# A spectral block on one core: TensorE's block order in the MLP slices, layer-2 chunks by twos and x's transposes moved to the inverse transform

## The chip, the cores and the metric

The kernel runs on one core of one Trainium2 chip. The metric is the device time in microseconds of one execution. Everything is float32. TensorE does the matrix products and the transpositions (a transposition is a matmul too), VectorE (DVE), ScalarE (ACT) and GpSimd (POOL) do the elementwise work, SyncE (SP) issues all DMAs.

## The reference, cut to what matters

The input x is 16 images of 56 x 56 positions with 64 channels. Two layers follow each other:

```
layer 0: whitening
  m, cov of the 64 channels over all 50,176 positions
  L = cholesky((1-eps) cov + eps I);  y = inv(L) (x - m) * gamma + beta
layer 1: residual = y
  h  = layer_norm(y) * g1 + b1
  xf = rfft2(h over rows and columns)
  o1 = relu(complex 8-block linear of xf);  o2 = softshrink(complex 8-block linear of o1, 0.01)
  r  = irfft2(o2) + h + residual
  n2 = layer_norm(r)
  out = gelu(n2 @ mw1 + mb1) @ mw2 + mb2 + r        (64 -> 256 -> 64 channels)
```

The Fourier transforms are done as matrix products with cosine and sine tables. Softshrink is computed as v - clamp(v, -0.01, 0.01).

## The kernel before, in words

The kernel first reads all images for the covariance and factors it. Then it goes through the images in eight pairs, one outer step each. Two images fill 112 of 128 partitions (2 x 56 rows).

A step i works on three pairs at once. For pair i it does the spectral part: dft_h, dft_w, layer_1, layer_2 (eight chunks), inv_w (the inverse column transform, eight chunks) and inv_h. For pair i-1 it does the MLP in seven slices of 8 columns. For pairs i+1 and i+2 it does the whitening and the transposes of x. The work of the last two is spread by hand among the rest; there is no planner, and each engine has its own program, kept in step with the others by semaphores. Step 0 has no MLP beside it (`behind` is false), steps 6 and 7 have no x to transpose (`ahead2` is false), and step 7 has no next pair (`ahead` is false). After step 7 comes the MLP of the last pair.

One slice of TensorE's program is `mlp(i, s, fill)` at line 1091. It calls mlp_in(s) (64 to 256 channels, line 1069), mlp_out(s-1) (256 to 64, line 1078), then fill(0), fill(1), transpose_n(s+1) (the n2 transposes, line 1060), fill(2), turn_out(s-1) (the MLP output turned back, line 1087), fill(3). The fills bring in the spectral work: in slices 1 and 2 the chunks 0 to 3 and 4 to 7 of layer_2 (line 1023), in slices 3 and 4 those of inv_w (line 1034). The table `X_BESIDE` says which of the seven blocks of x's transposes (line 953) follow which fill.

PSUM bank 3 (`BANK_M`) is used in turn by mlp_out(s-1), transpose_n(s+1) and turn_out(s-1). ScalarE empties it after the first two (ev_mlp_t, ev_n2), VectorE after the third: `ev_mlp` at line 701 reads the bank, adds the residual and writes `oslice`, line 707, which SP then stores. So the mlp_out of the next slice waits in `free_c` until ev_mlp is done.

Layer-2 chunks use banks 1 and 2 in turn. For each chunk VectorE adds the bias (line 692) and clamps (line 698), and POOL subtracts the two (line 436), with two buffers between VectorE and POOL. VectorE's slice_ at line 730 calls e0, e1, e2, then ev_mlp(s-1), then e3. In slices 1 and 2 the e's are the chunks, with the statistics of the next pair's layer norm behind some of them, seven bn_stats at a time (line 588): in slice 1 behind the second and the fourth chunk, in slice 2 behind the first, the second and the fourth. In slices 3 and 4 the e's hold the rest of that layer norm.

Slices 5 and 6 are not calls of mlp: in the tail of a step mlp_in(5), mlp_out(4), inv_h, transpose_n(6), turn_out(4), mlp_in(6) and mlp_out(5) are written out by hand. `mlp_order` (line 112) lists the use of the banks for the semaphore counts and has to follow the order of the calls.

Of the kernel before, what the change touches and what calls it, by code (L numbers as in the profile page):

```python
# [79 lines left out]

X_BESIDE = {1: [[0], [], [1], []], 2: [[2], [], [3], []], 3: [[4], [5], [6], []]}


def x_bank(i, k):
# [25 lines left out]
def mlp_order(i):  # L112

    order = [("n2", 0), ("n2", 1)] if last_pair(i) else [("n2", 0)]
    for s in range(SLICES):
        order += [("hid", s, m, v) for m in range(2) for v in range(2)]
        if last_pair(i):
            order += [("out", s - 2)] * (s > 1) + [("mlp", s - 1)] * (s > 0) + [("n2", s + 2)] * (s < SLICES - 2)
        else:
            order += [("mlp", s - 1)] * (s > 0) + [("n2", s + 1)] * (s < SLICES - 1) + [("out", s - 1)] * (s > 0)  # L120
    if last_pair(i):
        return order + [("mlp", SLICES - 1), ("out", SLICES - 2), ("out", SLICES - 1)]
    return order + [("mlp", SLICES - 1), ("out", SLICES - 1)]
# [44 lines left out]
def build(nc, x, consts, params, out):  # L168
# [5 lines left out]
    with ExitStack() as ctx:  # L174
# [151 lines left out]
        with nc.Block() as block:  # L326
# [123 lines left out]
            def _(dve):  # L450
# [279 lines left out]
                def step(i, ahead, behind):  # L730
                    def slice_(s, e0, e1, e2, e3):

                        e0()
                        e1()
                        e2()
                        if behind and s > 0:
                            ev_mlp(i - 1, s - 1)
                        e3()

                    def next_(what, *args):  # L740
                        if ahead:
                            what(i + 1, *args)

                    if behind:
                        ln2_stats(i - 1, 4)
                        if i > 1:
                            ev_mlp(i - 2, SLICES - 1)
                        for k in range(5, 8):
                            ln2_stats(i - 1, k)
                        ln2(i - 1)  # L750
                    next_(ev_whiten, [1] if behind else [0, 1])
                    ev_layer_1(i)
                    if i == 0:
                        folded_weights()
                    slice_(0, lambda: next_(ev_whiten, [2, 3, 4]), lambda: next_(ev_whiten, [5]),
                           lambda: next_(ev_whiten, [6]), lambda: next_(ln1_stats, [0]))
                    slice_(1, lambda: ev_layer_2(i, [0]), lambda: (ev_layer_2(i, [1]), next_(ln1_stats, [1])),
                           lambda: ev_layer_2(i, [2]), lambda: (ev_layer_2(i, [3]), next_(ln1_stats, [2])))
                    slice_(2, lambda: (ev_layer_2(i, [4]), next_(ln1_stats, [3])),
                           lambda: (ev_layer_2(i, [5]), next_(ln1_stats, [4])),  # L760
                           lambda: ev_layer_2(i, [6]), lambda: (ev_layer_2(i, [7]), next_(ln1_stats, [5])))
                    slice_(3, lambda: next_(ln1_stats, [6, 7]), lambda: next_(mean_rstd, 0),
                           lambda: next_(ln1_subtract, 0), lambda: None)
                    slice_(4, lambda: next_(ln1_rstd, 0), lambda: next_(ln1_subtract, 1), lambda: None,
                           lambda: next_(ln1_rstd, 1))
                    slice_(5, lambda: ev_inv_h(i, [0, 1]), lambda: None, lambda: ev_inv_h(i, [2, 3]), lambda: None)
                    if ahead:
                        slice_(6, lambda: ev_inv_h(i, [4, 5]), lambda: (ln2_stats(i, 0), ln2_stats(i, 1)),
                               lambda: ev_inv_h(i, [6, 7]), lambda: (ln2_stats(i, 2), ln2_stats(i, 3)))
# [44 lines left out]
            def _(pe):  # L814
# [213 lines left out]
                def inv_w(i, ks):  # L1028
                    for k in ks:

                        pe.wait_ge(y_ready, i * 8 + 4 * (k // 4) + 4)
                        t = free_b(i, INVW + k)
                        for j in range(4):
                            last = nc.tensor.matmul(t[:, j * 112:j * 112 + 112], y_v[:, 4 * k + j, :], cc("invw"),  # L1034
                                                    start=True, stop=True)
                        last.then_inc(pe_b, 1)
# [54 lines left out]
                def mlp(i, s, fill):  # L1091

                    mlp_in(i, s)
                    if s > 0:
                        mlp_out(i, s - 1)
                    fill(0)
                    fill(1)
                    if s < SLICES - 1:
                        transpose_n(i, s + 1)
                    fill(2)  # L1100
                    if s > 0:
                        turn_out(i, s - 1)
                    fill(3)

                def step(i, ahead, ahead2, behind):

                    def slice_(s, fill):
                        if behind:
                            mlp(i - 1, s, fill)
                        else:  # L1110
                            for j in range(4):
                                fill(j)

                    def whiten_next(j):
                        if ahead and j < 3:
                            whiten(i + 1, [4 + j])

                    def and_x(s, what):
                        def both(j):
                            what(j)  # L1120
                            if ahead2:
                                transpose_x(i + 2, X_BESIDE[s][j])
                        return both

                    dft_h(i)
                    if ahead:
                        whiten(i + 1, [0])
                    dft_w(i)
                    if ahead:
                        whiten(i + 1, [1])  # L1130
                    layer_1(i)
                    if i == 0:
                        folded_weights()
                    if ahead:
                        whiten(i + 1, [2])

                    pe.wait_ge(b_act, i * B_ACT + b_done("act", L2 - 1))
                    pe.wait_ge(b_dve, i * B_DVE + b_done("dve", L2 - 1))
                    if behind:
                        transpose_n(i - 1, 0)  # L1140
                    if ahead:
                        whiten(i + 1, [3])
                    slice_(0, whiten_next)
                    slice_(1, and_x(1, lambda j: layer_2(i, j)))
                    slice_(2, and_x(2, lambda j: layer_2(i, 4 + j)))
                    slice_(3, and_x(3, lambda j: inv_w(i, [j])))
                    slice_(4, lambda j: inv_w(i, [4 + j]))
                    if behind:
                        mlp_in(i - 1, 5)
                        mlp_out(i - 1, 4)  # L1150
                    inv_h(i, 0)
                    if behind:
                        transpose_n(i - 1, 6)
                    inv_h(i, 1)
                    if behind:
                        turn_out(i - 1, 4)
                        mlp_in(i - 1, 6)
                    inv_h(i, 2)
                    if behind:
                        mlp_out(i - 1, 5)  # L1160
                    if not ahead:
                        turn_out(i - 1, 5)
                        mlp_out(i - 1, 6)
                    inv_h(i, 3)
                    if behind:
                        turn_out(i - 1, 5 if ahead else 6)
# [34 lines left out]
            def _(act):  # L1201
# [94 lines left out]

                def mlp(i, s, fill):

                    gelu(i, s, 0)
                    gelu(i, s, 1)  # L1300
                    if s > 0:
                        ev_mlp_t(i, s - 1)
                    fill(0)
                    fill(1)
                    if s < SLICES - 1:
                        ev_n2(i, s + 1)
                    fill(2)
                    fill(3)

                def step(i, ahead2, behind):  # L1310
# [7 lines left out]
                    def x_next(s, j):  # L1318
                        if ahead2:
                            ev_x(i + 2, X_BESIDE[s][j])  # L1320

                    def first_inv_w(j):
                        ev_inv_w(i, [j])
                        x_next(3, j)

                    ev_dft_h(i)
                    ev_dft_w(i)
# [4 lines left out]
                    slice_(1, lambda j: x_next(1, j))  # L1332
                    slice_(2, lambda j: x_next(2, j))
                    slice_(3, first_inv_w)
                    slice_(4, lambda j: ev_inv_w(i, [4 + j]))
                    slice_(5, lambda j: None)
                    slice_(6, lambda j: None)

# [168 lines left out]
```

## Time and profile before

| | |
|---|---|
| median of 3 runs | 841.62 us (840.57 to 844.27) |
| profiled execution, its own time | 842.9 us |
| its span, first to last instruction | 841.1 us |
| mean granted TensorE clock | 0.932 |
| TensorE busy | 778.3 us (93%) |
| VectorE busy | 569.4 us (68%) |
| ScalarE busy | 378.4 us (45%) |
| GpSimd busy | 251.9 us (30%) |

Busy shares are averages over the whole span. In the rows below a block of equal instructions is merged to one line; the time from the start of one block to the start of the next is what a block takes, since a matmul's recorded end overlaps the next one. In brackets stands the idle time of the engine just before the block, with the instruction whose end released it.

### The profile page before, as it was taken

How to read it: one execution, taken by the hardware profiler on the slowest of the kernel's cores; microseconds unless marked ns; L12 is line 12 of the kernel's file. 1: busy time of each engine (PE TensorE's matmuls, PEld its weight loads, DVE VectorE, ACT ScalarE, POOL GpSimd, SP SyncE). 2: the span in 40 equal slices, each digit the busy share in tenths (PEclk: the TensorE clock that was granted, in tenths of full speed). 3: DMA queues.
4: the chain of work that ended last, by engine and by line, in shares of the span. 5: the costliest groups of instructions: out<-in, count | busy, mean ns of one | idle time of the engine just before them, and what ended most of it. 6: DMA issues, size and time to landing. Idle time of an engine off the chain costs nothing.

```text
span 841.1 us, 17115 instructions
## 1 busy us (share of the span) xinstructions
PE 778.3 (93%) x6823; PEld 542.9 (65%) x6823; DVE 569.4 (68%) x1860; ACT 378.4 (45%) x687; POOL 251.9 (30%) x107
## 2 busy tenths in 40 slices
PE   7999996986799999999999999999999998989987
PEld 5985555875477667666766667676757664746433
DVE  4567777279577767776776777677867695843551
ACT  0011005623164735563556455545554545455455
POOL 4000000932903270427042604360435045413000
PEclk9895557899699999999999999999999999999999
DMA  9943002002000121002100300030001001001012
GB/s 263 276 113 107 1 0 75 3 2 78 1 1 13 34 65 46 24 23 82 29 25 23 95 17 24 23 108 4 23 23 34 2 24 34 23 2 34 23 34 67
DMA packets 10369, 39.41 MB, mean 47 GB/s; under 512 B 1282, under 2 KB 1410, under 8 KB 8834
## 3 DMA queue, kind: packets, MB, share of 16 engines
q1 hardware_dynamic: 10290, 38.31, 15.8%
q8 instruction: 55, 0.90, 0.4%
q14 instruction: 24, 0.20, 0.1%
HBM read 25.46 MB, written 12.85 MB: 46 GB/s over the span
## 4 chain that ended last, share of the span: by engine, by line
PE 80%; DVE 15%; issue 3%; ACT 1%; DMA 0%; DVEq 0%; ACTq 0%
PE psum L1069 11%; PE psum L1078 10%; PE psum L982 7%; PE psum L1047 6%; PE psum L992 6%; PE psum L1023 6%; PE psum L1034 6%; PE psum L1007 6%; PE psum L966 5%; PE psum L829 4%; PE psum L886 4%; DVE stats L588 3%; PE psum L1087 3%; PE psum L953 2%; PE psum L1060 2%
## 5 line engine op out<-in xcount | busy, mean ns | idle before, releaser
L1271 ACT ACTIVATE hid<-psum,hbias 128x448 f32<-128x448 f32 x224 | 124.0, 636 | 80.6 <-PE psum L1069 80.6
L436 POOL TENSOR_TENSOR p_y<-layer,clamped 128x512 f32<-128x512 f32 x64 | 75.5, 1180 | 240.1 <-DVE clamped L698 240.1
L1069 PE MATMUL psum<-n2T,mw1s 64*128 64x448 f32 x448 | 102.7, 577 | 1.7 <-ACT n2T L1264 1.7
L1078 PE MATMUL psum<-hid,prm 128*64 128x448 f32 x448 | 96.3, 552 | 2.0 <-DVE oslice L707 2.0
L401 POOL TENSOR_TENSOR hbuf<-hbuf,prm 112x3584 f32<-112x3584 f32 x7 | 43.4, 6205 | 111.1 <-DVE hbuf L653 111.1
L1047 PE MATMUL psum<-u_r,cst 58*112 58x448 f32 x256 | 60.4, 592 | 15.5 <-DVE rbuf L720 11.3
L1023 PEld LDWEIGHTS psum<-w2s,o_g 128*64 128x64 f32 x1856 | 60.1, 138 | 15.5 <-issue 8.9
L692 DVE TENSOR_TENSOR layer<-psum,prm 128x512 f32<-128x512 f32 x64 | 40.4, 631 | 41.6 <-PE psum L1023 41.6
L1034 PEld LDWEIGHTS psum<-cst,p_y 128*128 128x128 f32 x512 | 61.2, 192 | 11.2 <-issue 5.6
L1023 PE MATMUL psum<-w2s,o_g 128*64 128x64 f32 x1856 | 66.3, 224 | 2.1 <-DVE layer L692 2.1
L1034 PE MATMUL psum<-cst,p_y 128*128 128x112 f32 x512 | 66.7, 277 | 1.2 <-DVE layer L692 1.2
L982 PE MATMUL psum<-cst,hbuf 112*112 112x116 f32 x512 | 57.1, 270 | 9.5 <-DVE hbuf L802 7.4
L672 DVE TENSOR_TENSOR ybuf<-psum,prm 112x512 f32<-112x512 f32 x49 | 33.9, 691 | 46.4 <-PE psum L966 45.8
L982 PEld LDWEIGHTS psum<-cst,hbuf 112*112 112x112 f32 x512 | 54.3, 182 | 16.6 <-issue 9.0
L1078 PEld LDWEIGHTS psum<-hid,prm 128*64 128x64 f32 x448 | 27.3, 136 | 58.4 <-issue 42.8
L966 PE MATMUL psum<-wy,xT 128*112 128x128 f32 x448 | 61.0, 287 | 3.8 <-DVE ybuf L672 3.0
L588 DVE BATCH_NORM_STATS2 stats<-ybuf 112x6 f32<-112x64 f32 x448 | 60.6, 212 | 3.7 <-ACT ybuf L1354 3.5
L966 PEld LDWEIGHTS psum<-wy,xT 128*112 128x112 f32 x448 | 54.7, 186 | 13.1 <-issue 13.1
L1214 ACT COPY u_r<-psum 112x464 f32<-112x464 f32 x64 | 35.0, 546 | 60.0 <-PE psum L982 60.0
L1069 PEld LDWEIGHTS psum<-n2T,mw1s 64*128 64x128 f32 x448 | 39.9, 190 | 30.1 <-issue 21.6
L992 PE MATMUL psum<-cst,u_r 112*128 112x116 f32 x464 | 53.3, 275 | 0.6 <-ACT u_r L1214 0.6
L1047 PEld LDWEIGHTS psum<-u_r,cst 58*112 58x112 f32 x256 | 23.2, 184 | 46.2 <-issue 45.3
(130 smaller groups left out, 1308.7 us busy)
## 6 DMA issues: line engine op xcount, KB each, us to landing
xin<-x_dram SPq DMA_DIRECT2D x8, 1568.0 KB, 8.3
out_dram<-oslice SPq DMA_DIRECT2D x56, 224.0 KB, 2.2
ybuf<-x_dram SPq DMA_DIRECT2D x2, 1568.0 KB, 16.8
fbuf<-x_dram SPq DMA_DIRECT2D x2, 1568.0 KB, 19.9
xin<-x_dram SPq DMA_DIRECT2D x4, 392.0 KB, 5.2
n<-x_dram SPq DMA_DIRECT2D x1, 1568.0 KB, 22.1
n<-x_dram SPq DMA_DIRECT2D x4, 392.0 KB, 15.7
prm<-params_dram SPq DMA_DIRECT2D x1, 742.0 KB, 3.9
```

Of the source, the lines that this page charges most:

```text
L436: nc.gpsimd.tensor_tensor(yk, a, b, ALU.subtract).then_inc(y_ready, 1)
L588: last = nc.vector.bn_stats(stats[:, w, :], src[:, w * C:(w + 1) * C])
L966: last = nc.tensor.matmul(t[0:ROWS, j * 128:(j + 1) * 128], xT[:, w * ROWS:(w + 1) * ROWS], wy[:], start=(i > 0), stop=True, skip_group_ch ...
L982: last = nc.tensor.matmul(t[0:ROWS, j * 2 * KR:(j + 1) * 2 * KR], h_w[:, 4 * k + j, :], cc("f1", ROWS), start=True, stop=True)
L992: last = nc.tensor.matmul(t[:, j * 4 * KF:(j + 1) * 4 * KF], u_r[0:ROWS, (4 * k + j) * 128:(4 * k + j + 1) * 128], cc("f2", ROWS), start=T ...
L1007: one = nc.tensor.matmul(t[b][:, 0:(z - a) * KF], w1s[C * b:C * b + C, 256 * s + 128 * half:256 * s + 128 * half + 128], p_v[C * b:C * b + ...
L1023: last = nc.tensor.matmul(t[C * r:C * r + C, j * C:j * C + C], o_g[:, at:at + C], w2s[:, 128 * half + C * r:128 * half + C * r + C], start ...
L1034: last = nc.tensor.matmul(t[:, j * 112:j * 112 + 112], y_v[:, 4 * k + j, :], cc("invw"), start=True, stop=True)
L1047: one = nc.tensor.matmul(t[d][0:ROWS, 0:7 * C], cc("invh")[rows, ROWS * m:ROWS * m + ROWS], g[rows], start=(m == 0), stop=(m == 1))
L1069: nc.tensor.matmul(t[:, 0:4 * ROWS], mw1s[C * v:C * v + C, HH * m:HH * m + HH], n2T[C * v:C * v + C, s % 2, :], start=True, stop=True).the ...
L1078: last = nc.tensor.matmul(t[C * v:C * v + C, 0:4 * ROWS], pp("mw2")[:, C * m:C * m + C], hid[:, s % 2, m, v, :], start=(m == 0), stop=(m = ...
L1271: nc.scalar.activation(hid[:, s % 2, m, v, :], bank[CH_MLP[i].bank[k]][:, 0:4 * ROWS], ACT.Gelu, bias=hbias[:, m:m + 1]).then_inc(c_act, 1)
```

## The change

The change moves instructions; it adds and removes none.

- `X_BESIDE`: the seven blocks of x's transposes were in slices 1, 2 and 3 (two, two and three of them). Now one is in slice 1, one in slice 2, three in slice 3 and two in slice 4. Within a fill an x block now comes ahead of the fill's other work instead of behind it.
- TensorE, slices 1 and 2: turn_out(s-1) comes behind fill(3) instead of ahead of it. With the emptied table entries the order of a slice is mlp_in, mlp_out, chunk, chunk, n2 transposes, x transposes, chunk, chunk, turn_out. VectorE's ev_mlp(s-1) moves behind e3 to match.
- The tail: mlp_out(4) comes ahead of mlp_in(5), and ScalarE's ev_mlp_t(4) ahead of the gelus of slice 5; `mlp_order` follows.

```
-X_BESIDE = {1: [[0], [], [1], []], 2: [[2], [], [3], []], 3: [[4], [5], [6], []]}
+X_BESIDE = {1: [[], [], [0], []], 2: [[], [], [1], []], 3: [[2], [], [3], [4]], 4: [[5], [], [6], []]}
...
 # VectorE, slice_
                         e2()
+                        if s in (1, 2):
+                            e3()
                         if behind and s > 0:
                             ev_mlp(i - 1, s - 1)
-                        e3()
+                        if s not in (1, 2):
+                            e3()
...
 # TensorE, mlp
                     fill(2)
+                    if s in (1, 2):
+                        fill(3)
+                        turn_out(i, s - 1)
+                        return
                     if s > 0:
                         turn_out(i, s - 1)
                     fill(3)
...
                         def both(j):
-                            what(j)
                             if ahead2:
                                 transpose_x(i + 2, X_BESIDE[s][j])
+                            what(j)
...
-                    slice_(4, lambda j: inv_w(i, [4 + j]))
+                    slice_(4, and_x(4, lambda j: inv_w(i, [4 + j])))
                     if behind:
+                        mlp_out(i - 1, 4)
                         mlp_in(i - 1, 5)
-                        mlp_out(i - 1, 4)
...
 # ScalarE, mlp
+                    if s == 5:
+                        ev_mlp_t(i, s - 1)
                     gelu(i, s, 0)
                     gelu(i, s, 1)
-                    if s > 0:
+                    if s not in (0, 5):
                         ev_mlp_t(i, s - 1)
...
 # ScalarE, step
                     def first_inv_w(j):
+                        x_next(3, j)
                         ev_inv_w(i, [j])
-                        x_next(3, j)
+
+                    def last_inv_w(j):
+                        x_next(4, j)
+                        ev_inv_w(i, [4 + j])
```

## Rows read from the trace of the kernel before

**Rows 1.** The page's chain that ended last, shares of the span by engine.
```profile
PE 80%; DVE 15%; issue 3%; ACT 1%; DMA 0%; DVEq 0%; ACTq 0%
```

**Rows 2.** TensorE's timeline (start us, length us, instructions), step 4, slices 1 and 2.
```profile
505.45 1.10 PE L1023 MATMUL psum<-w2s,o_g 128*64 128x64 f32 x32
...
509.71 0.60 PE L953 MATMUL psum<-cst,xin 112*128 112x112 f32 x4
510.15 0.60 PE L1087 MATMUL psum<-cst,mlp_t 128*112 128x128 f32 x4
...
511.42 1.77 PE L1069 MATMUL psum<-n2T,mw1s 64*128 64x448 f32 x8
513.12 1.72 PE L1078 MATMUL psum<-hid,prm 128*64 128x448 f32 x8
514.67 1.10 PE L1023 MATMUL psum<-w2s,o_g 128*64 128x64 f32 x32
```

**Rows 3.** TensorE's timeline, step 4, slices 3 and 4 and the tail's start.
```profile
522.34 1.72 PE L1078 MATMUL psum<-hid,prm 128*64 128x448 f32 x8
...
531.52 1.72 PE L1078 MATMUL psum<-hid,prm 128*64 128x448 f32 x8
...
536.33 0.60 PE L1087 MATMUL psum<-cst,mlp_t 128*112 128x128 f32 x4
...
537.74 1.77 PE L1069 MATMUL psum<-n2T,mw1s 64*128 64x448 f32 x8
```

**Rows 4.** VectorE's timeline, step 4, slices 1 to 4.
```profile
506.60 0.69 DVE L692 TENSOR_TENSOR layer<-psum,prm 128x512 f32<-128x512 f32 x1 [2.52 <-PE psum L1023]
507.32 0.43 DVE L698 TENSOR_SCALAR clamped<-layer 128x512 f32<-128x512 f32 x1
...
...
522.33 2.75 DVE L588 BATCH_NORM_STATS2 stats<-ybuf 112x6 f32<-112x64 f32 x21
...
530.55 0.68 DVE L707 TENSOR_TENSOR oslice<-psum,fbuf 112x512 f32<-112x512 f32 x1
...
536.96 0.69 DVE L707 TENSOR_TENSOR oslice<-psum,fbuf 112x512 f32<-112x512 f32 x1 [1.86 <-PE psum L1087]
```

**Rows 5.** VectorE's and POOL's timelines, step 0, layer-2 chunks and statistics.
```profile
182.23 0.68 DVE L692 TENSOR_TENSOR layer<-psum,prm 128x512 f32<-128x512 f32 x1
...
187.39 1.10 DVE L698 TENSOR_SCALAR clamped<-layer 128x320 f32<-128x320 f32 x1
...
189.31 0.67 DVE L692 TENSOR_TENSOR layer<-psum,prm 128x512 f32<-128x512 f32 x1
...
195.79 2.74 DVE L588 BATCH_NORM_STATS2 stats<-ybuf 112x6 f32<-112x64 f32 x21
...
187.04 1.28 POOL L436 TENSOR_TENSOR p_y<-layer,clamped 128x512 f32<-128x512 f32 x1 [0.67 <-DVE clamped L698]
```

**Rows 6.** TensorE's timeline, step 6, and VectorE's last write-back before the wait.
```profile
671.20 2.03 PE L1023 MATMUL psum<-w2s,o_g 128*64 128x64 f32 x64
673.17 0.60 PE L1060 MATMUL psum<-cst,n 112*128 112x112 f32 x4
...
695.97 1.72 PE L1078 MATMUL psum<-hid,prm 128*64 128x448 f32 x8 [1.78 <-DVE oslice L707]
...
695.23 0.68 DVE L707 TENSOR_TENSOR oslice<-psum,fbuf 112x512 f32<-112x512 f32 x1
```

**Rows 7.** TensorE in the last MLP; the windows row is length, busy, granted clock, DMA.
```profile
810.60 0.60 PE L1060 MATMUL psum<-cst,n 112*128 112x112 f32 x4 [2.37 <-DVE n L631]
811.13 3.18 PE L1069 MATMUL psum<-n2T,mw1s 64*128 64x448 f32 x8
...
811.00:813.00 2.00, 2.00 (x9) 0.59 0.00 0
```

**Rows 8.** VectorE's write-back and TensorE's mlp_out behind it, step 7, slices 1 and 2.
```profile
756.94 0.67 DVE L707 TENSOR_TENSOR oslice<-psum,rbuf 112x512 f32<-112x512 f32 x1
...
758.02 1.72 PE L1078 MATMUL psum<-hid,prm 128*64 128x448 f32 x8
```

More of the change, by code:

```diff
@@ L115, in mlp_order @@
     for s in range(SLICES):
+        if s == 5 and not last_pair(i):
+            order += [("mlp", 4)]
         order += [("hid", s, m, v) for m in range(2) for v in range(2)]
@@ L119, in mlp_order @@
         else:
-            order += [("mlp", s - 1)] * (s > 0) + [("n2", s + 1)] * (s < SLICES - 1) + [("out", s - 1)] * (s > 0)
+            order += [("mlp", s - 1)] * (s not in (0, 5)) + [("n2", s + 1)] * (s < SLICES - 1) + [("out", s - 1)] * (s > 0)
     if last_pair(i):
@@ L1334, in step @@
                     slice_(3, first_inv_w)
-                    slice_(4, lambda j: ev_inv_w(i, [4 + j]))
+                    slice_(4, last_inv_w)
                     slice_(5, lambda j: None)
```

## The prediction, made before the result was known

> **What bounds the kernel now.** I read the page first, then TensorE's instructions in order of time, then VectorE's, then TensorE's granted clock by windows. The chain that ended last is 80% TensorE and 15% VectorE [rows 1], so what counts is TensorE's order and each place where it waits. I call a pass of the outer loop a step. Steps 1 to 5 repeat each other to a hundredth of a microsecond, 82.88 us apart; the rows are of step 4. In its slices 1 to 4 TensorE doesn't wait at all [rows 2, 3]. Step 6 has no x to transpose: there the same TensorE work is shorter, VectorE's is not, and mlp_out of slice 3 waits 1.78 us for VectorE's write-back `oslice` [rows 6]. That is the wait to watch. mlp_out writes bank 3, which the previous slice's out transposes used too, so it needs the VectorE read of that bank (ev_mlp) to be over.
>
> **Slices 1 and 2, TensorE.** All x transposes but one per slice go, and the rest of the order is mlp_in, mlp_out, chunk, chunk, n2, x, chunk, chunk, turn_out. Spacings, start to start: two adjacent chunks 1.97 us (step 6, [rows 6]); a transposition block before another 0.44 (510.15 - 509.71), a transposition block and the short last chunk together 1.27 (511.42 - 510.15), mlp_in 1.70 [rows 2]. Turn_out straight before mlp_in isn't in the rows; it lies between the 0.44 and its recorded length of 0.60, I take 0.53. From the first chunk to the point where the next mlp_out could start: 1.97 (two chunks) + 0.44 (n2) + 1.27 (x and the last chunk) + 0.98 (the third chunk) + 0.53 + 1.70 = 6.9 us. Before it was 513.12 - 505.45 = 7.67. So TensorE alone would gain 0.77 us a slice.
>
> **Slices 1 and 2, VectorE.** What is moved here is more than TensorE's blocks. turn_out(s-1) now comes after the fourth chunk, and ev_mlp(s-1) in VectorE's queue after e3, which is the last chunk's add and clamp and then seven statistics. Before, ev_mlp stood ahead of e3, and turn_out ahead of the last chunk. Now mlp_out of the next slice waits for all of it. The chunk's add starts 1.15 us after its matmuls start [rows 2, 4]. From there on VectorE has work without a break, and step 0 shows exactly this sequence, since it has no ev_mlp in it [rows 5]: from the first add of slice 1 to the first add of slice 2 it is 189.31 - 182.23 = 7.08 us. ev_mlp then takes its place at the end, and mlp_out starts 0.74 us after ev_mlp starts [rows 6]. Slice 1: 1.15 + 7.08 + 0.74 = 8.97 us against 7.67: 1.30 later, with a TensorE wait of 8.97 - 6.9 = 2.1 us. Slice 2 has two more groups of statistics between the chunks: 195.79 - 189.31 = 6.48 to the statistics of e3, 0.90 for seven of them (a third of that row's 21), so 1.15 + 6.48 + 0.90 + 0.74 = 9.27 against 522.34 - 514.67 = 7.67: 1.60 later, a wait of 2.4 us.
>
> The 7.08 holds an effect that step 4 didn't have: a clamp that starts while POOL subtracts lasts until POOL has finished. The clamp of 320 columns at 187.39 took 1.10 us beside POOL's subtraction of 187.04 to 188.32 [rows 5]; the full clamp of 512 columns at 507.32 took 0.43 [rows 4]. With chunks far apart the clamps fell between the subtractions, with chunks by twos they don't. In the Trainium skill, SBUF — State Buffer, section "SBUF: two separate sides", the port pair of VectorE and GpSimd is an exclusive lock held for a whole instruction. By that rule, the trace agrees; without it three clamps a step would be some 0.6 us shorter each, which is a rival below.
>
> **Slices 3 and 4.** Slice 3 has three x blocks before and after; I take nothing for it. VectorE is not late there: from the statistics at 522.33 to ev_mlp at 530.55 it is 8.22 us [rows 4], 0.90 less now that seven statistics are over before ev_mlp(1), 0.68 more for ev_mlp itself, 8.0 against TensorE's 531.52 - 522.34 = 9.18 [rows 3]. Slice 4 gets two x blocks that had been in slices 1 and 2: 2 x 0.44 = +0.88 us, uncovered, since TensorE is the bound there. This is the point of the balance: x's transposes leave a stretch where VectorE decides the end and go to one where TensorE does.
>
> **Tail.** mlp_out(4) now stands ahead of mlp_in(5), so it lacks the 1.70 us that covered ev_mlp(3). That starts at 536.96, 0.63 after turn_out, so the bank is free 0.63 + 0.74 = 1.37 after turn_out starts; TensorE gets there after 537.74 - 536.33 = 1.41 [rows 3, 4]. It just fits: 0, with up to 0.1 a step on top. ScalarE's turned order there and x's later copies to xT (needed a step later) cost nothing: ScalarE is busy 45% of the span by the page. SP's queue doesn't change its order, and the next load of x stands behind stores that come later than the moved blocks.
>
> **Sum.** Steady step: +1.30 + 1.60 + 0 + 0.88 = +3.78, five times: +18.9. Step 0: its slices 1 to 4 are VectorE's already, and TensorE waits later for it anyway: 0. Step 6, first chunk to mlp_out of slice 3: 8.97 + 1.55 (mlp_out to chunk, [rows 2]) + 9.27 + 7.98 (9.18 less three x blocks, about 1.2) = 27.77 against 695.97 - 671.20 = 24.77: +3.0; here the old 1.78 us wait is used up by the new ones. Step 7 has no statistics: ev_mlp comes later by the last chunk's add, about 0.5 (0.69 for a full one, [rows 4]), and its held clamp, 189.31 - 187.39 less the 0.90 of statistics = 1.02 [rows 5], 1.5 in all, of which 758.02 - 756.94 - 0.74 = 0.34 was slack [rows 8]: +1.2 in each of two slices, +2.4. Together +24.3 us.
>
> **TensorE's clock.** The new waits are 2.1 and 2.4 us in five steps, 2.5 and 2.8 in step 6: twelve that are over 2 us. At 810.60 a single wait of 2.37 us stood behind a busy stretch, and the clock fell: 0.59 in the next 2 us, the lower of the two levels (1.2 GHz) for most of it, and an mlp_in took 3.18 us instead of 1.77 [rows 7]. After the wait of 1.78 us at 695.97 the next block was at full speed, 1.72 [rows 6]. The new waits lie between and above. A fall costs 3.18 - 1.77 = 1.4 us in that block and a little in its neighbour; I estimate 1.5. It counts in full, for what follows each wait (mlp_out and the first chunk) starts VectorE's next sequence. The bounds are 0 and 12 x 1.5 = 18; I take 10 of 12, since the nearest row to 2.4 us is the one that fell: +15.
>
> The Trainium skill speaks against this: TensorE: Matmul & The Clock Gate, "Part 1: The HAM clock gate", has the clock fall after an idle stretch that is longer than each of the new waits. By it the time would be that of the first rival; the fall behind 2.37 us in this trace is against it.
>
> So +24.3 + 15 = +39.3 on the profiled execution's 842.9 us (span 841.1): 882.2. That execution lies 1.3 above the median of 841.62, so **881 us**.
>
> **Rivals.**
> 1. The same waits, but the clock stays up, as behind 1.78 us: 841.6 + 24.3 = 866. Against it stands the fall after 2.37. Chance 0.20.
> 2. The clamps aren't held, since POOL's subtractions fall otherwise, and then the waits are shorter and end at full clock: three clamps x 0.6 = 1.8 less in five steps, about 1.2 less each in steps 6 and 7: 866 - 11.2 = 855. For it: in step 4 they weren't held. Chance 0.05.
> 3. The other side: ev_mlp is in time, TensorE never waits for it, and the grouping pays. Then a steady step is 2 x (6.9 + 1.55 - 9.22) + 0.88 = -0.66, step 6 loses its wait too (22.5 against 24.77, -2.3), step 7 -0.2: -5.8 in all, 836. It decides by one gap: ev_mlp must be over by the end of the next mlp_in, 2.2 us after the last chunk lands (0.53 + 1.70); the add, clamp and statistics ahead of it and itself come to over 2.5 even from an idle VectorE. Chance 0.05.
> 4. All twelve waits bring a fall and some of them two stretches of low clock in succession, as the low clock lasted through step 0's tail: 892 to 905. Chance 0.08.
>
> **Numbers.** My forecast, between eight and all twelve falls, 873 to 891, has 0.62. The range takes in the first rival: 862 to 892. About 0.5% (4 us) is what a measurement can tell from no change: faster 0.05 (rival 3), within it 0.02, slower 0.93.
>
> **What would show it.** Right: mlp_out waits of 2 to 3 us with `oslice` as their releaser, in slices 2 and 3 of steps 1 to 6, some 1.3 in step 7; clamps of 1.0 to 1.1 us in steps 1 to 5; granted clock at one half behind most of the waits; slice 4 longer by 0.9; ev_mlp right behind e3's statistics. Wrong: no such waits (rival 3), waits at full clock (rival 1), clamps of 0.43 (rival 2), or a new wait in the tail before mlp_out(4).

## The result, and the profile after

The changed kernel took 862.14 us (median of 4 runs, 861.28 to 863.51) against 842.94 for the kernel before beside it (4 runs, 840.57 to 846.08): a ratio of 1.024, 95% interval 1.021 to 1.027, so 2.4% slower. The profiled execution took 861.5 us with a span of 859.7, 18.6 over the span before. I had forecast 881, with 862 to 892 as the range: the direction is right, but the slowdown is about half of what I forecast. The time lies 0.1 us inside the range's lower edge, next to my first rival ("the same waits, but the clock stays up", 866) and outside my forecast proper (873 to 891).

The page of the changed kernel: the chain of waits by engine, which answers to [rows 1], and mlp_out's group (busy us, mean ns, idle us just before and its releaser):
```profile
PE 70%; DVE 23%; issue 5%; POOL 1%; ACT 1%; DMA 0%; DVEq 0%; ACTq 0%
...
L1083 PE MATMUL psum<-hid,prm 128*64 128x448 f32 x448 | 96.9, 554 | 28.8 <-DVE oslice L709 28.8
```
TensorE's share of the chain fell from 80% to 70% and VectorE's rose from 15% to 23%. TensorE is idle for 28.8 us in front of mlp_out, released by the write-back `oslice`: 14 waits, two in each of steps 1 to 7. Before there were two such waits in the whole program, the 1.78 us of [rows 6] the longer.

TensorE's timeline of the changed kernel, step 4 (start us, length us, instructions, [idle before <- releaser]), which answers to [rows 2, 3]:
```profile
513.88 2.04 PE L1028 MATMUL psum<-w2s,o_g 128*64 128x64 f32 x64
515.84 0.60 PE L1065 MATMUL psum<-cst,n 112*128 112x112 f32 x4
516.28 0.55 PE L958 MATMUL psum<-cst,xin 112*128 112x112 f32 x4
516.76 1.74 PE L1028 MATMUL psum<-w2s,o_g 128*64 128x64 f32 x52
518.42 0.65 PE L1092 MATMUL psum<-cst,mlp_t 128*112 128x128 f32 x4
519.00 1.77 PE L1074 MATMUL psum<-n2T,mw1s 64*128 64x448 f32 x8
522.83 1.73 PE L1083 MATMUL psum<-hid,prm 128*64 128x448 f32 x8 [2.06 <-DVE oslice L709]
524.39 2.04 PE L1028 MATMUL psum<-w2s,o_g 128*64 128x64 f32 x64
...
533.65 1.72 PE L1083 MATMUL psum<-hid,prm 128*64 128x448 f32 x8 [2.34 <-DVE oslice L709]
...
542.70 1.72 PE L1083 MATMUL psum<-hid,prm 128*64 128x448 f32 x8
...
549.65 1.72 PE L1083 MATMUL psum<-hid,prm 128*64 128x448 f32 x8
551.31 1.77 PE L1074 MATMUL psum<-n2T,mw1s 64*128 64x448 f32 x8
```
The order is the new one: two chunks in one block (x64), n2 and x, two chunks (x52, the last is short), turn_out, mlp_in. The first wait is 2.06 us, the second 2.34; slice 3 to slice 4 has none, and neither has the tail. The mlp_outs shown are mlp_out(1), (2), (3) and (4) at 522.83, 533.65, 542.70 and 549.65; each stands at the start of the slice behind its own. "mlp_out of slice 3", here and in the prediction, is mlp_out(3).

VectorE's timeline of the same slice, which answers to [rows 4], and POOL's subtraction beside its last clamp:
```profile
515.02 0.69 DVE L694 TENSOR_TENSOR layer<-psum,prm 128x512 f32<-128x512 f32 x1 [2.52 <-PE psum L1028]
...
516.81 1.01 DVE L700 TENSOR_SCALAR clamped<-layer 128x512 f32<-128x512 f32 x1
...
520.20 1.10 DVE L700 TENSOR_SCALAR clamped<-layer 128x320 f32<-128x320 f32 x1
521.22 0.97 DVE L590 BATCH_NORM_STATS2 stats<-ybuf 112x6 f32<-112x64 f32 x7
522.11 0.67 DVE L709 TENSOR_TENSOR oslice<-psum,fbuf 112x512 f32<-112x512 f32 x1
...
519.85 1.27 POOL L438 TENSOR_TENSOR p_y<-layer,clamped 128x512 f32<-128x512 f32 x1 [0.67 <-DVE clamped L700]
```
From 515.02 VectorE works without a break until the write-back at 522.11, which mlp_out waits for; it starts 0.72 us after it. Two clamps in this slice take over 1.0 us; the last of them ends at 521.30, 0.2 us behind POOL's subtraction (519.85 + 1.27 = 521.12).

Now the clock. TensorE alone, windows of 6 us (length, busy, granted clock, DMA share, GB/s): one ahead of step 0's chunks, which the table below needs, and three from mlp_outs that had waited:
```profile
174.00:180.00 6.00, 4.43 (x48) 1.00 0.00 0
435.55:441.55 6.00, 6.00 (x80) 0.72 0.13 40
522.83:528.83 6.00, 6.00 (x132) 1.00 0.13 38
619.82:625.82 6.00, 6.00 (x34) 0.72 0.13 38
```
Behind the wait that ends at 522.83 the clock stays at 2.4 GHz. Of the windows behind the twelve new waits it fell to 1.2 GHz for part of two only: behind the first wait of step 3 and the second of step 5. The timeline shows the price there: at 437.39 the two chunks took 3.33 us, in place of 2.04.

Where the span's 18.6 us are, by the start of the first layer-2 chunk of each step:

| stretch | before | after | difference |
|---|---|---|---|
| start to step 1 | 256.82 | 254.24 | -2.58 |
| step 1 to 6, steps without a fall | 82.88 each | 86.18 each | +3.30 each, +16.5 |
| extra in the steps 3 and 5, with a fall | | 87.27, 87.77 | +2.7 |
| step 6 | 80.22 | 81.68 | +1.46 |
| step 7 to the end | 89.7 | 90.2 | +0.5 |

The first row isn't the change's: another execution of the changed kernel reached step 1 at 256.72, and over the twelve profiles of this case the start lies between 252.1 (experiment 6) and 257.6, with low stretches of TensorE's clock at other places (174 to 180 us: 1.00 here, 0.72 in the execution of before). The step-to-step distances are free of that, so the experiments are read by them.

### The profile page after: what moved, and what is told of

The parts are those of the page before. It is cut to its first block, busy times and chain, and to the rows that moved or that the text cites. A ratio compares the mean times of both kernels' runs of the same rounds, so it can differ in the third digit from the quotient of the medians.

```text
span 859.7 us, 17115 instructions
## 1 busy us (share of the span) xinstructions
PE 772.0 (90%) x6823; PEld 542.4 (63%) x6823; DVE 581.2 (68%) x1860; ACT 376.5 (44%) x687; POOL 251.6 (29%) x107
## 4 chain that ended last, share of the span: by engine, by line
PE 70%; DVE 23%; issue 5%; POOL 1%; ACT 1%; DMA 0%; DVEq 0%; ACTq 0%
PE psum L1083 10%; PE psum L1074 8%; PE psum L987 7%; PE psum L997 6%; PE psum L1039 6%; PE psum L1052 6%; DVE stats L590 6%; PE psum L1012 5%; PE psum L971 5%; DVE layer L694 4%; PE psum L834 3%; PE psum L891 3%; DVE clamped L700 2%; PE psum L1092 2%; PE psum L958 2%
## 5 line engine op out<-in xcount | busy, mean ns | idle before, releaser
L1083 PE MATMUL psum<-hid,prm 128*64 128x448 f32 x448 | 96.9, 554 | 28.8 <-DVE oslice L709 28.8
L1052 PE MATMUL psum<-u_r,cst 58*112 58x448 f32 x256 | 58.2, 574 | 14.5 <-DVE rbuf L722 10.3
L1289 ACT ACTIVATE mlp_t<-psum,prm 128x448 f32<-128x448 f32 x56 | 35.5, 634 | 71.1 <-PE psum L1083 69.6
L1028 PE MATMUL psum<-w2s,o_g 128*64 128x64 f32 x1856 | 62.8, 227 | 3.6 <-DVE layer L694 3.6
```

The lines of the kernel that those rows point to most:

```text
L1028: last = nc.tensor.matmul(t[C * r:C * r + C, j * C:j * C + C], o_g[:, at:at + C], w2s[:, 128 * half + C * r:128 * half + C * r + C], start ...
L1052: one = nc.tensor.matmul(t[d][0:ROWS, 0:7 * C], cc("invh")[rows, ROWS * m:ROWS * m + ROWS], g[rows], start=(m == 0), stop=(m == 1))
L1083: last = nc.tensor.matmul(t[C * v:C * v + C, 0:4 * ROWS], pp("mw2")[:, C * m:C * m + C], hid[:, s % 2, m, v, :], start=(m == 0), stop=(m = ...
```

## The experiments

**1. The change with VectorE's write-back put back ahead of e3** (and nothing else different). This is the one edit that my working made responsible.
```
-                        if s in (1, 2):
-                            e3()
                         if behind and s > 0:
                             ev_mlp(i - 1, s - 1)
-                        if s not in (1, 2):
-                            e3()
+                        e3()
```


> The changed kernel with VectorE's ev_mlp(s-1) back ahead of e3 in slices 1 and 2; TensorE's new order and x's new places stay. Theory (VectorE's order makes the waits): the waits of 2.06 and 2.34 us before mlp_out of slices 2 and 3 go. TensorE needs 6.9 + 1.55 us for each of slices 1 and 2 (before 9.22), VectorE's write-back is ready at 6.1 + 0.74 = 6.8. In slice 3 VectorE is now late instead, by some 0.7 us, for its layer-norm chain from chunk 4 to the write-back is 15.9 + 0.74 = 16.6 against TensorE's 16.0. Per steady step -0.77 -0.77 -0.13 +0.67 +0.73 -0.17 = -0.4, in all 2 to 3 us below the kernel before: about 840. Rival (the blocks by twos and x among the inverse transform cost by themselves): the time stays at 855 or more.

Measured 835.5 us (834.2 to 837.2), ratio 0.991 [0.988, 0.995]; step 82.36. TensorE's timeline of this kernel, slice 2 and the mlp_out of slice 3:
```profile
509.87 2.03 PE L1025 MATMUL psum<-w2s,o_g 128*64 128x64 f32 x64
...
516.73 1.72 PE L1080 MATMUL psum<-hid,prm 128*64 128x448 f32 x8
...
526.50 1.72 PE L1080 MATMUL psum<-hid,prm 128*64 128x448 f32 x8 [0.64 <-DVE oslice L709]
```
The first chunk to mlp_out is 516.73 - 509.87 = 6.86 us, my TensorE sum of 6.9, with no wait. One line of VectorE's order makes 3.82 of the 86.18 us of a step, and turns a kernel 2.4% slower into one 0.9% faster. Of that 0.9% the new order itself has only a part: of the 8.6 us between this execution's span (832.5) and that of before (841.1), 2.6 are the five steady steps'; 2.4 lie ahead of step 1, which differs between executions anyway, and 1.5 in step 6 and 2.1 in step 7 and the last MLP, mostly from falls of the clock that lie otherwise. What is left is a wait of 0.64 us in slice 3, where VectorE is now late.

**2. The other way round: the kernel before, with only that order changed.**
```
+                        if s in (1, 2):
+                            e3()
                         if behind and s > 0:
                             ev_mlp(i - 1, s - 1)
-                        e3()
+                        if s not in (1, 2):
+                            e3()
```


> The kernel before with one edit: VectorE's ev_mlp(s-1) behind e3 in slices 1 and 2. TensorE's order, x's places and the tail are those of before. Theory: each of the two slices ends with VectorE's add, clamp, seven statistics and write-back behind the last chunk, mlp_out waits some 1.6 us twice a steady step: +16 in five steps, +3 in step 6, +2 in step 7, about 864, the whole loss of the changed kernel and more. Rival (TensorE's new order is what costs): 843 to 846.

Measured 861.5 us (859.7 to 864.1), ratio 1.022 [1.019, 1.026]; step 85.76. TensorE's timeline of this kernel, step 4, and the longest wait of step 6:
```profile
514.62 1.10 PE L1026 MATMUL psum<-w2s,o_g 128*64 128x64 f32 x32
...
523.57 1.72 PE L1081 MATMUL psum<-hid,prm 128*64 128x448 f32 x8 [1.22 <-DVE oslice L707]
...
695.07 2.74 PE L1081 MATMUL psum<-hid,prm 128*64 128x448 f32 x8 [2.29 <-DVE oslice L707]
```
The order alone brings +2.88 us a step, nearly all of the change's +3.30. First chunk to mlp_out is 523.57 - 514.62 = 8.95 us, the same as in the changed kernel: VectorE's sequence sets it whichever way TensorE's blocks lie, and the wait is shorter (1.22, 1.52) only because more of TensorE's work fills the slice. From the first add to the write-back it is 7.09 us here too. VectorE does idle in between, 0.46 and 0.19 us for chunks that come later, but its second and last clamp start later beside POOL's subtractions and end just behind them all the same: they take 0.46 and 0.81 us in place of 1.01 and 1.10. Behind the wait at 695.07 the clock fell, and mlp_out took 2.74 us.

**3 and 4. The x transposes alone, and the tail alone**, each in the kernel before. The first is the new `X_BESIDE` with what reads it, the second puts mlp_out(4) ahead of mlp_in(5).
```
-X_BESIDE = {1: [[0], [], [1], []], 2: [[2], [], [3], []], 3: [[4], [5], [6], []]}
+X_BESIDE = {1: [[], [], [0], []], 2: [[], [], [1], []], 3: [[2], [], [3], [4]], 4: [[5], [], [6], []]}
```


> The kernel before with x's transposes in their new places (one, one, three and two in slices 1 to 4, each ahead of the fill's work), and nothing else. Theory: slices 1 and 2 shorten by about 0.7 us each since VectorE's write-back is in time at 6.5 to 6.8 us, slice 4 lengthens by 0.7, and slice 3 gets a wait of about 0.6 for the write-back behind VectorE's layer-norm chain: -0.2 a step, 840 to 843. Rival (x's two blocks in slice 4 are a pure loss, and slices 1 and 2 don't gain): +0.7 a step, 846 to 847.

```
+        if s == 5 and not last_pair(i):
+            order += [("mlp", 4)]
...
-                        mlp_in(i - 1, 5)
                         mlp_out(i - 1, 4)
+                        mlp_in(i - 1, 5)
```


> The kernel before with only the tail's part of the change: mlp_out(4) ahead of mlp_in(5), ScalarE's ev_mlp_t(4) ahead of the gelus of slice 5. To be read from the distance of one step's first layer-2 chunk to the next one's (82.88 us in the kernel before). Theory (from the changed kernel's trace, where the tail was 0.17 us shorter): 82.7, since mlp_in ahead of inv_h takes less than mlp_out does, and ev_mlp(3) is just in time. Rival (the cover of 1.70 us is missing, as bounded in the prediction): a wait before mlp_out(4) of up to 0.1, 82.9 to 83.0.

The first took 842.8 us (839.5 to 844.5), ratio 1.000 [0.998, 1.002], step 82.69: -0.19. It has a wait of 0.50 us in slice 3: TensorE leaves slices 1 and 2 earlier, and VectorE comes no sooner. The second took 842.6 us (one execution); its step is 82.69 too, -0.19, without a new wait. So neither is to blame, and each gives back a little. With experiment 1 the grouping of the chunks is worth 82.36 - 82.88 + 0.38 = -0.14 a step, if the three add up (no run has the grouping alone). Slice 3's wait, 0.50 here and 0.64 in experiment 1, is in these values.

**5. The change, with e3's seven statistics moved behind the write-back.**
```
                         if s in (1, 2):
                             e3()
                         if behind and s > 0:
                             ev_mlp(i - 1, s - 1)
+                        if s in (1, 2):
+                            next_(ln1_stats, [2 if s == 1 else 5])
```


> The changed kernel with the seven statistics of e3 moved behind ev_mlp in slices 1 and 2; the last chunk's add and clamp stay ahead of it. Theory (the wait is the sum of what stands ahead of the write-back in VectorE's queue): each of twelve waits shortens by the 0.89 us of seven statistics, 2.06 to 1.17 and 2.34 to 1.44; step 7 stays as it is: -10.7, about 851.5. Rival (the wait is set by POOL's subtraction or by ScalarE): unchanged at 862.

Measured 852.8 us (851.4 to 854.4), ratio 1.011 [1.007, 1.015]; step 84.40. TensorE's timeline of this kernel, the two mlp_outs of step 4 that wait:
```profile
518.66 1.72 PE L1085 MATMUL psum<-hid,prm 128*64 128x448 f32 x8 [1.17 <-DVE oslice L709]
...
528.58 1.72 PE L1085 MATMUL psum<-hid,prm 128*64 128x448 f32 x8 [1.45 <-DVE oslice L709]
```
Each wait is shorter by the 0.89 us that the statistics take, and the step by twice that (1.78). What stands between the last chunk's add and the write-back goes into the time one for one. None of its waits for the write-back was followed by a fall of the clock.

**6. The change, with POOL's subtraction cut short** (64 columns in place of 512), to free VectorE's clamps from it. This kernel leaves out the rest of the softshrink.
```
-    nc.gpsimd.tensor_tensor(yk, a, b, ALU.subtract)
+    nc.gpsimd.tensor_tensor(yk[:, 0:1], a[:, 0:1], b[:, 0:1], ALU.subtract)
```


> The changed kernel with POOL's subtraction cut to one of up to eight columns' groups of each chunk (the rest of the shrunk sum is left out), so POOL is done with each chunk in about 0.2 us and not 1.3. Nothing waited for the subtraction's end by itself. Theory (a clamp that starts while POOL subtracts is held until POOL ends): the three clamps of 1.0 to 1.1 us a step take 0.43 and 0.51, the waits shrink by 1.17 in slice 1 (2.06 to 0.9) and 0.59 in slice 2 (2.34 to 1.75), -11 in steps 1 to 6 and -2 to -3 in step 7, about 848. Rival (these clamps are slow for another reason, such as the order of VectorE's own instructions): clamps and time unchanged, 862.

Measured 841.5 us (841.1 to 846.7), ratio 1.001 [0.999, 1.003]; step 84.07. VectorE's and POOL's timelines of this kernel, step 4, slice 1:
```profile
507.23 0.43 DVE L700 TENSOR_SCALAR clamped<-layer 128x512 f32<-128x512 f32 x1
...
510.04 0.33 DVE L700 TENSOR_SCALAR clamped<-layer 128x320 f32<-128x320 f32 x1
...
507.74 0.33 POOL L438 TENSOR_TENSOR p_y<-layer,clamped 128x64 f32<-128x64 f32 x1 [0.73 <-DVE clamped L700]
```
The clamps are 0.43 and 0.33 us in place of 1.01 and 1.10, and the waits 0.71 and 1.56: shorter by 1.35 = 0.58 + 0.77, and by 0.77. Two thirds of a first wait are the time in which VectorE is held by POOL. The Trainium skill has VectorE and GpSimd share a port pair as an exclusive lock for a whole instruction (SBUF — State Buffer, "SBUF: two separate sides"); by that rule a clamp that starts beside a subtraction can't end before it, and here the trace agrees, 1.10 with it and 0.33 without. The time is 6.5 us below what I expected here. Of the 20.1 us between the two profiled spans (859.7 and 839.6) 10.6 are the five steady steps', 2.7 the falls that went, 2.1 step 6, 2.6 step 7 and the end, and 2.1 lie ahead of step 1 (252.1 us), where step 0 has held clamps too [rows 5] and the clock was low for less time. I had counted neither the falls nor step 0.

**7. The change with longer waits**: seven more statistics, written to a spare tile, ahead of the write-back in slices 1 and 2.
```
+                        if ahead and behind:
+                            for w in range(7):
+                                nc.vector.bn_stats(spare[:, i, at + w, :], ybuf[:, w * C:(w + 1) * C])
```


> The changed kernel with seven more statistics (of columns that are not needed, into a spare tile) ahead of the write-back in slices 1 and 2 of steps 1 to 6. The twelve waits grow by 0.89 to 2.95 and 3.2 us. Without the clock: +10.7, 873. Theory on the clock (the longer the wait, the surer the fall; 2.1 to 2.3 us is near the edge, so two of twelve fell): most of the twelve are followed by a stretch of low granted clock, +10 to +15 more, 880 to 888. Rival (a fall depends on where a wait lies in time, not on its length): again two or three falls, 873 to 877.

Measured 882.3 us (882.1 to 882.5, two runs), ratio 1.048 [1.044, 1.051]. TensorE alone, windows of 6 us behind the first and the second wait of step 1, and the mlp_out of a wait in step 3:
```profile
264.46:270.46 6.00, 6.00 (x132) 1.00 0.14 41
276.16:282.16 6.00, 6.00 (x34) 0.72 0.13 38
...
443.51 2.97 PE L1089 MATMUL psum<-hid,prm 128*64 128x448 f32 x8 [2.94 <-DVE oslice L710]
```
The waits are 2.8 to 3.3 us long, and now the clock falls behind 8 of 12. They also lie at other times than before, so the length isn't the only thing that differs.

**8. The changed kernel again, unaltered**, to see whether the falls keep their places.

> The changed kernel, unaltered, once more. Both theories: 862 and waits of 2.06 and 2.33 us. If what comes before a wait in the program decides whether the clock falls, the falls stand where they stood: behind the first wait of step 3 and the second of step 5. If it is the wait's place in time against something that doesn't keep step with the program, they stand elsewhere, and their number can differ.

It took 865.0 us (two runs), ratio 1.027 [1.024, 1.031]. The falls came in the same two places. TensorE's timeline of this execution:
```profile
438.01 2.17 PE L1083 MATMUL psum<-hid,prm 128*64 128x448 f32 x8 [2.06 <-DVE oslice L709]
439.96 3.23 PE L1028 MATMUL psum<-w2s,o_g 128*64 128x64 f32 x64
...
622.40 2.23 PE L1083 MATMUL psum<-hid,prm 128*64 128x448 f32 x8 [2.33 <-DVE oslice L709]
```
Two executions are few, but it speaks for something in the program's course, and against chance, as what picks the waits.

**9. The best version: experiment 1, with slice 3's write-back put ahead too** (of e2), where experiment 1 had its 0.64 us.
```
+                        if s == 3 and behind:
+                            ev_mlp(i - 1, s - 1)
                         e2()
-                        if behind and s > 0:
+                        if behind and s > 0 and s != 3:
                             ev_mlp(i - 1, s - 1)
```
(Experiment 1's edit is in it as well.)

> The changed kernel with VectorE's ev_mlp ahead of e3 in slices 1 and 2, and in slice 3 also ahead of the layer norm's first subtraction (e2). In slice 3 turn_out(2) is there before VectorE's chain of small operations ends, so VectorE doesn't wait for it, and the write-back comes 1.94 us earlier (the subtraction's time). Theory: the last wait of 0.64 us before mlp_out of slice 3 goes in five steps and that of 1.8 in step 6: 5 us below the 835.5 of the kernel with only the first part, about 831. Rival (the layer norm's later end delays POOL's scaling and with it the next dft_h): no gain, 835 or more.

Measured 832.0 us (830.9 to 834.4, 6 runs), ratio 0.988 [0.986, 0.990]: 1.2% faster than the kernel before, 3.5% than the changed one. Step 81.65. TensorE's timeline of this kernel, mlp_out of the slices 1 to 3 after the first chunks of slice 1, no wait among them:
```profile
502.50 2.03 PE L1027 MATMUL psum<-w2s,o_g 128*64 128x64 f32 x64
...
509.33 1.72 PE L1082 MATMUL psum<-hid,prm 128*64 128x448 f32 x8
...
517.74 1.72 PE L1082 MATMUL psum<-hid,prm 128*64 128x448 f32 x8
...
526.79 1.73 PE L1082 MATMUL psum<-hid,prm 128*64 128x448 f32 x8
```

**10. That version, with two x blocks back between the third and fourth chunks of slices 1 and 2.**
```
-X_BESIDE = {1: [[], [], [0], []], 2: [[], [], [1], []], 3: [[2], [], [3], [4]], 4: [[5], [], [6], []]}
+X_BESIDE = {1: [[], [], [0], [1]], 2: [[], [], [2], [3]], 3: [[4], [], [5], [6]], 4: [[], [], [], []]}
```


> The kernel with both write-backs ahead (81.65 us a step) and x's two blocks of slice 4 back in slices 1 and 2, one each, between the third and the fourth layer-2 chunk; slice 3 has three as there. VectorE makes TensorE wait nowhere in either. Theory (a transposition block beside layer-2 chunks takes more of TensorE than one among the inverse column transform's): 0.53 and a worse chunk boundary of 0.1 against 0.37, +0.5 for the two, 82.1 us a step. Rival (it costs the same wherever it stands): 81.65.

It took 834.9 us (one execution); step 82.25, +0.60 for the same instructions. TensorE's timeline of this kernel, the second half of slice 1:
```profile
505.25 1.15 PE L1027 MATMUL psum<-w2s,o_g 128*64 128x64 f32 x32
506.33 0.60 PE L957 MATMUL psum<-cst,xin 112*128 112x112 f32 x4
506.87 0.80 PE L1027 MATMUL psum<-w2s,o_g 128*64 128x64 f32 x20
507.60 0.65 PE L1091 MATMUL psum<-cst,mlp_t 128*112 128x128 f32 x4
```
Chunk, x, chunk is 507.60 - 505.25 = 2.35 us, against 518.42 - 516.76 = 1.66 for the two chunks without it: the block costs 0.69 here, 0.3 more than where the change puts it (0.37, from slice 4's lengths below).

## Why the prediction was right, and where it was wrong

- **Slices 1 and 2: right.** First chunk to mlp_out 8.97 and 9.27 us forecast, 8.95 and 9.26 measured; waits 2.1 and 2.4 against 2.06 and 2.34. The sequence of step 0 [rows 5] was the right one to read, held clamps included: from the first add to the write-back 7.08, measured 7.09. Experiments 1, 2 and 5 show that the place of the write-back in VectorE's queue does it.
- **The other side (rival 3): excluded by the waits themselves.** It needed VectorE's write-back over by the end of the next mlp_in, and that came 2.06 and 2.34 us too late. With the write-back put ahead it is in time, and the gain comes (-0.52 a step, -1.23 with slice 3 mended; I had worked out -0.66).
- **Clamps not held (rival 2): excluded** for this kernel; experiment 6 prices the holding at 2 x 0.77 + 0.58 = 2.1 us a step, where I had 1.8, since the short clamp alone takes 0.33, which no row had shown. So the short clamps of step 4 before, 0.52 and 0.51 us, were held a little already, against what I wrote under rival 2.
- **Slice 3: -0.13 in place of 0, slice 4: +0.73 in place of +0.88, tail: -0.17 in place of 0.** Three sizes taken too high. In slice 4 the two x blocks came to 0.37 each; I had taken 0.44 from an x block that stands before another transposition [rows 2]. The step that failed is the spacing, read off in other company; my own sum for step 6 had three x blocks among inv_w at 1.2, 0.40 each. The steady step is +3.30, not +3.78.
- **Step 6: right**, +2.92 us to slice 3's mlp_out for +3.0 (waits 2.44, 2.33); the row in the table has only +1.46, as the execution of before had a stretch of low clock there that the changed one has not (1.3 us), and the tail gained 0.17. TensorE's timeline of before, behind step 6:
```profile
741.94 0.58 PE L1060 MATMUL psum<-cst,n 112*128 112x112 f32 x4 [1.47 <-ACT o_g L1249]
743.14 3.42 PE L1069 MATMUL psum<-n2T,mw1s 64*128 64x448 f32 x8 [0.62 <-ACT n2T L1264]
```
In the changed execution the same mlp_in stands behind the same two waits, 1.47 and 0.62 us, and took 1.84.
- **Step 7: right**, +2.33 for +2.4, from the first chunk to mlp_out(2). The row in the table has only +0.5, since the fall of [rows 7] lies behind the wait for n, where it lengthens the chain. The changed execution has a fall there too, but it comes ahead of that wait and is taken in by it, 1.03 us in place of 2.37:
```profile
822.47 3.35 PE L1074 MATMUL psum<-n2T,mw1s 64*128 64x448 f32 x8
...
830.81 0.60 PE L1065 MATMUL psum<-cst,n 112*128 112x112 f32 x4 [1.03 <-DVE n L633]
```
- **TensorE's clock: this term failed.** I had it fall behind 10 of the 12 waits, at 1.5 us each, +15. It fell behind 2, and cost 1.09 and 1.60 us in their steps, 2.7. The size of one fall was right, the count was not. I chose it by the nearest row, a single fall behind 2.37 us [rows 7], against a single wait of 1.78 without one [rows 6], and treated as a yes or no of the length what isn't one. The trace before had a row against it: the fall at 743.14 above, behind two waits of only 1.47 and 0.62 us. Counted over all twelve profiles, waits of mlp_out for the write-back were followed by a low clock in none of 43 of 1.0 to 1.8 us; in 5 of 26 of 1.9 to 2.6 us (two in each execution of the changed kernel, where the second repeats the first's places, and one in experiment 2); in 8 of 12 of 2.8 to 3.3 us (experiment 7). Rate and length go together, but behind one of 2.06 us it fell and behind one of 2.59 it didn't. The Trainium skill (TensorE: Matmul & The Clock Gate, "Part 1: The HAM clock gate") has the fall come after an idle stretch longer than any of these; by that rule the time would have been rival 1's 866, near the 862 measured. But that this comes near doesn't make the rule right here: the 5 and the 8 falls are against it.

That 862.1 lies inside the range at all is luck: the lower edge had been drawn 4 us below the first rival. The mechanism, the waits and their lengths, was right; the clock's term was not. Against the 882.2 forecast for the profiled execution, 20.7 us are missing: 12.3 are the clock's term, 2.4 the sizes in the steady steps (5 x 0.48), 1.5 step 6, 1.9 step 7 and the end, and 2.6 the course ahead of step 1, which differs between executions anyway.

Open: what picks the waits behind which the clock falls. Their places repeat in two executions, in experiment 7 the first wait of step 1 stayed at 1.00 and the second fell, and once the first wait of a step has brought a fall the second is shorter (1.88 us for 2.33 in step 3). Outside the count above it fell behind pairs of short waits, and in one execution and not in the other. No experiment here tells what TensorE did earlier that decides.

## What to carry to other kernels

When blocks of one engine are regrouped, follow what the moved block's reader does in the next engine's queue: here one write-back placed behind an add, a clamp and seven statistics cost 3.8 us a step, while the regrouping itself, the transposes' move and the tail each gave 0.1 to 0.2, and 1.23 together once slice 3's write-back was put ahead too. Put the operation that releases the bottleneck's buffer first in the other engine's queue, and the rest behind it. A fall of the clock behind a wait is a rate and not a yes or no: one row that fell is no reason to charge all of them.

## What the runs showed of the hardware

- A clamp of 512 columns takes 0.43 us alone and 1.01 beside POOL's subtraction; one of 320 takes 0.33 and 1.10, and ends 0.2 us behind POOL. The chunks by twos bring the first under a subtraction (1.01 in experiment 1 too), the late write-back the second: the clamp of 320 took 0.51 us in experiment 1, 0.81 in experiment 2's slice 1, 1.10 with both.
- The same transposition block costs TensorE 0.37 us among 112-column matmuls and 0.69 between two 64-column chunks, both as the difference with and without it; start to start it takes 0.44 to 0.48 next to another transposition.
- A wait of mlp_out of 1.9 to 2.6 us in work that is otherwise dense brought a low clock 5 times in 26 (0.72 over the 6 us behind it), at a price of 1.1 to 1.6 us where I took the difference of the steps.
